# A fused attention and ternary feed-forward kernel on one core: the last group's first MLP placed inside the sixth group's third stage, the f1 bias products in two parts, the last norm's variance in one-input passes, and a new order of all engines

## The reference

```python
x = x + attn(layernorm(x))
x = x + ffn(layernorm(x))

def attn(x):                                   # 256 features, 64 for Q and K
    n = layer_norm(x) * ln1_w + ln1_b
    Q, K = elu(n @ q_w.T + q_b) + 1, elu(n @ k_w.T + k_b) + 1
    V = n @ v_w.T + v_b
    a = causal_linear_attention(Q, K, V)       # sum over earlier tokens, divided by sum(q * k)
    x = x + a @ o_w.T + o_b
    h = gelu((layer_norm(x) * ln2_w + ln2_b) @ f1_w.T + f1_b)   # exact gelu
    return x + h @ f2_w.T + f2_b               # f1: 256 -> 1024, f2: 1024 -> 256

def ffn(x):
    h = gelu(x @ absmean(W_fc).T)              # absmean: weights of -1, 0 and 1
    h = layernorm(h) * ln_w + ln_b             # over 1024 features
    return h @ absmean(W_proj).T
```

## Time and profile before

| | us |
|---|---|
| median of 3 runs | 448.62 (448.35 to 449.17) |
| profiled execution, its own time | 450.32 |
| span of the profiled execution | 448.5 |
| PE busy in the span | 425.4 |
| before the first matmul | 6.42 |
| from the last matmul's end to the end of the span | 7.8 |

### The profile page before, as it was taken

The page is one execution under the profiler, slowest core; times in us unless marked ns, Lnnn a source line. Parts: engine busy times, 40 slices in busy tenths (PEclk is TensorE's granted clock), DMA queues, the critical chain, the costliest instruction groups (busy, mean ns, idle before and its releaser), DMA issues. The chain is left out here.

```text
span 448.5 us, 9187 instructions
## 1 busy us (share of the span) xinstructions
PE 425.4 (95%) x2910; PEld 388.0 (87%) x2910; DVE 361.1 (81%) x1156; ACT 324.6 (72%) x578; POOL 300.5 (67%) x268
## 2 busy tenths in 40 slices
PE   4999999999999999999999999999999999999892
PEld 3888888988989898988999899898989998989782
DVE  6797996886897888968897889978797858946686
ACT  4889558987498758986588847988388857963490
POOL 3684068596778559876689946895878521677384
PEclk9999998999999999999999999999999999999897
DMA  7324030100410021020301120120300000010011
GB/s 241 124 95 142 0 96 1 31 20 0 142 47 3 1 94 50 0 96 11 87 0 48 50 71 2 41 79 1 95 1 2 1 1 0 1 48 3 1 47 50
DMA packets 13521, 20.44 MB, mean 46 GB/s; under 512 B 2720, under 2 KB 11040, under 8 KB 12960
## 3 DMA queue, kind: packets, MB, share of 16 engines
q1 hardware_dynamic: 13472, 19.84, 13.7%
HBM read 15.62 MB, written 4.22 MB: 44 GB/s over the span
## 5 line engine op out<-in xcount | busy, mean ns | idle before, releaser
L1475 POOL TENSOR_TENSOR h<-h 128x512 f32<-128x512 f32 x56 | 72.5, 1295 | 8.8 <-ACT h L851 4.2
L292 PE MATMUL bank_y<-wf_hi,h_hi 128*128 128x256 f32 x224 | 63.4, 283 | 0.8 <-DVE h_lo L1091 0.6
L551 PE MATMUL bank_y<-wpj_t,g_hi 128*128 128x256 f32 x256 | 63.3, 284 | 0.1
L294 PE MATMUL bank_y<-wf_hi,h_lo 128*128 128x256 f32 x224 | 62.6, 279 | 0.0
L293 PE MATMUL bank_y<-wf_lo,h_hi 128*128 128x256 f32 x224 | 62.6, 279 | 0.0
L551 PE MATMUL bank_y<-wpj_t,g_lo 128*128 128x256 f32 x256 | 62.2, 280 | 0.0
L1453 POOL TENSOR_TENSOR rs<-ve,neg_half 128x2 f32<-128x2 f32 x32 | 22.5, 703 | 49.7 <-DVE ve L1028 45.8
L1091 DVE TENSOR_TENSOR h_lo<-bank_f,h_hi 128x512 fp32r<-128x512 f32 x45 | 30.5, 686 | 26.1 <-ACT h_hi L806 25.9
L551 PEld LDWEIGHTS bank_y<-wpj_t,g_hi 128*128 128x128 f32 x256 | 48.1, 188 | 2.2 <-issue 0.5
L551 PEld LDWEIGHTS bank_y<-wpj_t,g_lo 128*128 128x128 f32 x256 | 48.2, 188 | 1.2
L797 ACT ACTIVATE bank_f<-bank_f,f_bias 128x512 f32<-128x512 f32 x48 | 31.6, 662 | 20.0 <-PE bank_f L294 19.6
(11 more groups left out here) (330 smaller groups left out, 1471.3 us busy)
## 6 DMA issues: line engine op xcount, KB each, us to landing
out<-y_yc SPq DMA_DIRECT2D x15, 256.0 KB, 2.3
lines_b<-lines SPq DMA_DIRECT2D x6, 512.0 KB, 3.9
u<-in_xt SPq DMA_DIRECT2D x6, 512.0 KB, 3.6
x_even<-in_x SPq DMA_DIRECT2D x8, 256.0 KB, 2.9
x_odd<-in_x SPq DMA_DIRECT2D x8, 256.0 KB, 3.0
h<-in_f SPq DMA_DIRECT2D x1, 1024.0 KB, 7.7
y_yc<-in_f SPq DMA_DIRECT2D x1, 1024.0 KB, 10.0
h<-in_fc SPq DMA_DIRECT2D x1, 1024.0 KB, 6.1
```

Of the source, the lines that this page charges most:

```text
L292: pe.matmul(ps, w[0], r[0], start=start, stop=False, skip_group_check=skip)
L294: return pe.matmul(ps, w[1], r[0], start=False, stop=stop, skip_group_check=skip)
L551: mm = pe.matmul(out_half(t), gr[part][:, (8 * g + m) % RG, t * P:(t + 1) * P], wpj[:, m, :], start=(m == 0 and part == 0 and t % 2 == 0), ...
L1475: pool.tensor_tensor(squares[:, 0, :], squares[:, 0, :], square_tile(m), ALU.add).then_inc(s["squares_sum"], 1)
```

## The change

Five things are changed.

1. `fill` is gone. `f1b` has two parts: part 0 (m = 0 to 4, ten matmuls) stands where `fill` stood, part 1 (m = 5 to 7, six matmuls) behind `scores(0)`. `f1_bias_add` has two parts as well. `v_mm(0, 0)` now waits for the first of them, and the load of W_proj waits for part 1, which ends earlier than `f1b` did.
2. At ACT's start the gelu table is touched once and the order is another: a further table load (exp) stands ahead of `qk_exp(0)`, and all four `abs_part` stand ahead of the second `z2_norm` of group 0. The `gelu_table` call of group 6 is gone.
3. The ring goes by slot numbers. For groups 0 to 5 they are the same. Group 7's eight f1 tiles now stand between fc tiles 3 and 4 of group 6; fc tiles 4 and 5 follow in the middle of f2(7), tile 6 behind its first half, tile 7 behind its second. `tsq(6)` writes another bank.
4. The last norm: `square` scales by 1/32, so that the sum of the 1024 squares is their mean. A new `ln4_mean` (four operations for the mean and four for its square less eps) stands right behind `h_sum`, and `ln4_var` has four operations in place of twelve; the four of the mean in `centre(g, 0)` are gone.
5. All five lists are written in another order. In groups 1 to 7 the attention tiles and `tz3` of the group before now alternate: `attend(g, 0)`, `tz3(g-1, 0)`, `attend(g, 1)`, `tz3(g-1, 1)`, `attend(g, 2)` (in group 1 `tz3(0, 0)` and `tz3(0, 1)` lie round `attend(1, 3)`).

The diff, cut to its core:

```diff
+        def f1_slot(g, m):
+
+            return 18 * g + m - (0 if g < G - 1 else KH - EARLY)
+
+        def z3_slot(g, h):
+
+            return 18 * g + 8 + h
+
+        def fc_slot(g, m):
+
+            return 18 * g + 10 + m + (KH if g == G - 2 and m >= EARLY else 0)
...
+        def square_bank(g):
+
+            return bank_a[0] if g == G - 2 else bank_a[1]
...
-            def f1b():
-                pe.wait_ge(s["f1_loaded"], 16)
-                pe.wait_ge(s["vec_loaded"], 16)
-                pe.wait_ge(s["v_lo"], 1)
-                for m in range(KH):
+            def f1b(part):
+                if part == 0:
+                    pe.wait_ge(s["f1_loaded"], 16)
+                    pe.wait_ge(s["vec_loaded"], 16)
+                else:
+                    pe.wait_ge(s["v_lo"], 1)
+                for m in (range(FIRST), range(FIRST, KH))[part]:
                     for k in range(KD):
                         mm = pe.matmul(bank_y[0][:, m * BW:(m + 2) * BW], f1_raw[:, k, m * P:(m + 1) * P],
                                        ln2b_c[:, k:k + 1].to_broadcast([P, 2 * BW]),
@@ -390,13 +411,6 @@
                                 k == 0, k == KD - 1)
                 mm.then_inc(s["qk_done"], 1)
 
-            def fill():
-
-                pe.wait_ge(s["wqk_hi"], KD)
-                pe.wait_ge(s["wf1_hi"], 1)
-                for _ in range(10):
-                    pe.matmul(bank_y[1][:], wqk[0][:, 0, :], wf1[0][:, 0, 0:512], start=True, stop=True)
-
...
+                    if h == 0:
+                        pe.wait_ge(s["f1_bias_ready"], 1)
...
+            def slot_free(n):
+
+                for g in range(G):
+                    for m in range(KH):
+                        if f1_slot(g, m) == n - 3:
+                            pe.wait_ge(s["h_lo"], 8 * g + m + 1)
+                        if fc_slot(g, m) == n - 3:
+                            pe.wait_ge(s["g_lo"], 8 * g + m + 1)
+                            pe.wait_ge(s["h_added"], 8 * g + m + 1)
...
-                        pe.wait_ge(s["f1_bias_ready"], 1)
+                        pe.wait_ge(s["f1_bias_ready"], 2)
...
             def tsq(g):
 
                 pe.wait_ge(s["squares_sum"], 7 * g + 7)
-                pe.wait_ge(s["z2_lo"], 2 * min(g + 1, G - 1) + 1)
+                if g != G - 2:
+                    pe.wait_ge(s["z2_lo"], 2 * min(g + 1, G - 1) + 1)
+                else:
+                    pe.wait_ge(s["h_total"], g + 1)
                 for t in range(T):
-                    mm = pe.transpose(bank_a[1][:, t * P:(t + 1) * P], squares[:, 0, t * P:(t + 1) * P], ident[:])
+                    mm = pe.transpose(square_bank(g)[:, t * P:(t + 1) * P], squares[:, 0, t * P:(t + 1) * P], ident[:])
                 mm.then_inc(s["sq_done"], 1)
 
             def ths(g):
 
                 pe.wait_ge(s["h_added"], 8 * g + 8)
-                pe.wait_ge(s["xa_ready"], 4 * min(g + 1, G - 1) + 2)
+                pe.wait_ge(*((s["xa_ready"], 4 * g + 6) if g < G - 1 else (s["h2_total"], G - 1)))
...
-                qkb(); tu(0, 0); tu(0, 1); wvo_mm(); qk_mm(0); bvo(); fill(); tu(1, 0); v_mm(0, 0); v_mm(0, 1)
-                tu(1, 1); scores(0); qk_mm(1); attend(0, 0); attend(0, 1); attend(0, 2); attend(0, 3); f1b()
...
+                qkb(); tu(0, 0); tu(0, 1); wvo_mm(); qk_mm(0); bvo(); f1b(0); v_mm(0, 0); tu(1, 0); v_mm(0, 1)
+                tu(1, 1); scores(0); f1b(1); qk_mm(1); attend(0, 0); attend(0, 1); attend(0, 2); attend(0, 3)
...
+                fch(6, 1, 1); fch(6, 1, 0); fc(6, 2); attend(7, 3); fc(6, 3); proj(6, 0); proj(6, 1); tz2(7, 0)
+                proj(6, 2); tz2(7, 1); proj(6, 3); f1h(7, 0, 0); f1h(7, 0, 1); f1h(7, 1, 1); f1h(7, 1, 0); f1(7, 2)
+                f1(7, 3); f1(7, 4); f1(7, 5); f2(7, 0, 1); f2(7, 1, 1); f1(7, 6); f1(7, 7); f2(7, 0, 0); f2(7, 1, 0)
+                fc(6, 4); fc(6, 5); f2(7, 2, 0); f2(7, 3, 0); f2(7, 4, 0); f2(7, 5, 0); f2(7, 6, 0); f2(7, 7, 0)
+                fc(6, 6); f2(7, 2, 1); f2(7, 3, 1); f2(7, 4, 1); f2(7, 5, 1); f2(7, 6, 1); f2(7, 7, 1); fc(6, 7)
+                proj(6, 4); proj(6, 5); tz3(7, 0); ths(6); tz3(7, 1); proj(6, 6); tsq(6); fch(7, 0, 0); fch(7, 0, 1)
+                proj(6, 7); fch(7, 1, 0); fch(7, 1, 1); fc(7, 2); fc(7, 3); proj(7, 0); fc(7, 4); proj(7, 1); fc(7, 5)
+                proj(7, 2); fc(7, 6); proj(7, 3); fc(7, 7); proj(7, 4); proj(7, 5); proj(7, 6); ths(7); tsq(7)
+                proj(7, 7)
...
-                if g == 0 and m == 0:
-                    act.wait_ge(s["f1_bias_ready"], 1)
-                act.activation(f1_bank(m)[:], f1_bank(m)[:], ACT.Gelu, bias=f1_bias[:, m:m + 1]).then_inc(s["h_gelu"], 1)
+                if g == 0 and m in (0, FIRST):
+                    act.wait_ge(s["f1_bias_ready"], 1 if m == 0 else 2)
...
-                act.activation(square_tile(m), fc_bank(m)[:], ACT.Square).then_inc(s["squared"], 1)
+                act.activation(square_tile(m), fc_bank(g, m)[:], ACT.Square, scale=1.0 / 32).then_inc(s["squared"], 1)
...
+                tables(); gelu_table(); ln3_hi(); wqk_hi(); u_norm(0, 0); u_norm(0, 1); u_hi(0, 0); u_hi(0, 1)
+                wvo_copy(); wf1_hi(0); wf1_hi(1); wf1_hi(2); qk_exp(0); wvo_hi(); u_norm(1, 0); u_norm(1, 1); qk_hi(0)
...
-            def f1_bias_add():
-                dve.wait_ge(s["f1b_done"], 1)
-                dve.tensor_tensor(f1_bias[:], bank_y[0][:, 0:KH * BW:BW], f1b_c, ALU.add).then_inc(s["f1_bias_ready"], 1)
+            def f1_bias_add(part):
+                ms = (slice(0, FIRST), slice(FIRST, KH))[part]
+                dve.wait_ge(s["f1b_done"], part + 1)
+                dve.tensor_tensor(f1_bias[:, ms], bank_y[0][:, ms.start * BW:ms.stop * BW:BW], f1b_c[:, ms],
+                                  ALU.add).then_inc(s["f1_bias_ready"], 1)
...
                 dve.wait_ge(s["sq_done"], g + 1)
                 if g:
                     dve.wait_ge(s["ln4_ve"], 4 * g)
-                dve.tensor_reduce(h2_total[:], bank_a[1][:].rearrange("p (t f) -> p t f", t=T),
+                dve.tensor_reduce(h2_total[:], square_bank(g)[:].rearrange("p (t f) -> p t f", t=T),
                                   AXX, ALU.add).then_inc(s["h2_total"], 1)
 
             def h_sum(g):
 
+                dve.wait_ge(s["hs_done"], g + 1)
                 if g:
                     dve.wait_ge(s["h_mean"], 4 * g)
-                    dve.wait_ge(s["h_mean2"], 4 * g)
-                dve.wait_ge(s["hs_done"], g + 1)
                 dve.tensor_reduce(h_total[:], bank_a[0][:].rearrange("p (t f) -> p t f", t=T),
                                   AXX, ALU.add).then_inc(s["h_total"], 1)
 
+            def ln4_mean(g):
+
+                dve.wait_ge(s["h_total"], g + 1)
+                if g:
+                    dve.wait_ge(s["centred"], 4 * g)
+                    dve.wait_ge(s["ln4_ve"], 4 * g)
+                for t in range(T):
+                    dve.tensor_scalar(h_mean[:, t:t + 1], h_total[:, t:t + 1], -1.0 / H, None, ALU.mult).then_inc(s["h_mean"], 1)
+                dve.wait_ge(s["h_mean"], 4 * g + 4)
+                for t in range(T):
+                    dve.tensor_scalar(h_less[:, t:t + 1], h_mean[:, t:t + 1], h_mean[:, t:t + 1], LN_EPS,
+                                      ALU.mult, ALU.subtract).then_inc(s["h_less"], 1)
+
             def ln4_var(g):
 
-                dve.wait_ge(s["h_total"], g + 1)
-                for t in range(T):
-                    dve.tensor_scalar(h_mean2[:, t:t + 1], h_total[:, t:t + 1], h_total[:, t:t + 1], -1.0 / (H * H),
-                                      ALU.mult, ALU.mult).then_inc(s["h_mean2"], 1)
                 dve.wait_ge(s["h2_total"], g + 1)
-                dve.wait_ge(s["h_mean2"], 4 * g + 4)
+                dve.wait_ge(s["h_less"], 4 * g + 4)
                 if g:
                     dve.wait_ge(s["ln4_rs"], g)
                 for t in range(T):
-                    dve.tensor_scalar(ve[3][:, t:t + 1], h2_total[:, t:t + 1], 1.0 / H, h_mean2[:, t:t + 1],
-                                      ALU.mult, ALU.add).then_inc(s["h_var"], 1)
-                dve.wait_ge(s["h_var"], 4 * g + 4)
-                for t in range(T):
-                    dve.tensor_scalar(ve[3][:, t:t + 1], ve[3][:, t:t + 1], 0.0, LN_EPS, ALU.max, ALU.add).then_inc(s["ln4_ve"], 1)
+                    dve.tensor_scalar(ve[3][:, t:t + 1], h2_total[:, t:t + 1], h_less[:, t:t + 1], LN_EPS,
+                                      ALU.subtract, ALU.max).then_inc(s["ln4_ve"], 1)
 
             def centre(g, t):
...
 
-                if t == 0:
-                    dve.wait_ge(s["h_total"], g + 1)
-                    if g:
-                        dve.wait_ge(s["centred"], 4 * g)
-                    for n in range(T):
-                        dve.tensor_scalar(h_mean[:, n:n + 1], h_total[:, n:n + 1], -1.0 / H, None, ALU.mult).then_inc(s["h_mean"], 1)
...
+                h_add(7, 7); g_lo(7, 7); h_sum(7); ln4_mean(7); h2_sum(7); centre(7, 0); ln4_var(7); centre(7, 1)
```

(1 more changed line is left out.)

557 lines of the change are left out of this document (270 added, 287 removed).

## The result

The changed kernel takes 451.65 us (median of 4 runs, 450.81 to 451.99), the kernel before beside it 448.80 (448.35 to 449.17). The ratio is 1.0059, with a 95% interval of 1.0042 to 1.0075: it is slower by 0.6%, where 445.5 and so faster was forecast; it lies above the whole stated range, which ended at 450.5. The profiled execution took 451.74 us with a span of 449.9; of before it was 450.32 and 448.5.

What follows compares the result with a forecast made beforehand. PE was taken as the bound, busy 425.4 of 448.5 us. Terms -0.3 - 1.2 - 1.6 + 1.1 - 1.1 = -3.1 took the median 448.62 to 445.5 (own range 443.3 to 447.6; whole range 441.5 to 450.5).

Steps and rivals of the forecast that it cites:

- The first term: Start of the kernel: PE idle time added, partly given back later; sum -0.3 us, between -2.5 and +4.
- The hole: Start, group 0: PE idle from about 30.6 to 34.9 us waiting for ACT's z2, then some 1.5 more; +2.7 us.
- the half clock at 66 to 74 us: Slow matmuls behind a 1.1 us wait for z3, expected to go as attend(1, 3) fills the wait; 1.7 us.
- the third term: Last two groups up to gelu3(7, 0): interleaved work covers waits and slow clock, new waits open; -1.6 us, bounds -4 to +1.
- The second term: Middle groups: alternating attention and tz3 covers waits at 170.12 and 374.52; -1.2 us, between -2.7 and +0.3.
- The fourth: Last stage: POOL is the bound, with ln4_rstd(6), two outputs and seven sq_add in its chain; +1.1 us, 0 to +3.
- The fifth: Tail from tsq(7) to the last output: fewer small operations ahead of the power; -1.1 us, between -1.5 and -0.4.
- the slow one: Start: PE leaves the idle time at 30.6 to 34.9 at half clock; start +4, total 449.8 us; chance 0.17.
- The table rival: Start: ACT stands as long again behind the new load ahead of qk_exp(0), about 1.3 later; 446.8 us; chance 0.05.

## Why the prediction was wrong

**The first term, the start: -0.3 forecast, +4.0 in the traces.** Its first half held. The hole was forecast at 30.6 to 34.9 and came at about 30.8 to 35.0 in two waits; the first f1h was forecast at 40.8 and came at 41.08. Part 0 of f1b hid in the wait for wvo_lo, and `v_mm(0, 0)` came 0.40 later, for 0.15 to 0.25. What failed is the sentence on what is given back: "one new wait for `h_lo` of 0.45 remains: -1.1". By `f1(0, 7)` 1.2 of the 3.0 were indeed given back; then 4.2 were lost up to `f2(0, 7, 1)`. The run with ternary(3) moved has the same PE order, no wait and no fall of the clock, and takes 7.0 us there; the changed kernel takes 11.3. Of these 4.3, 2.65 are the wait of 2.50 with its restart and 1.66 the half clock behind it. The walk, that is the new lists gone through call by call with the durations of before, had priced the ternary calls by the time they took before, 2.05 each, where nothing ran on POOL; in the changed kernel they take 2.97, 2.97 and 2.91. The trace of before had no row of this operation beside a large POOL operation, and the step named no queue behind the three calls on DVE. The runs bear this out: ternary(3) moved gives 3.3 us, POOL's xs(0) moved gives 2.1. Both the longer calls and their place in the queue are needed for the wait: one call moved out of the queue ended it though the others stayed slow (2.20 for a select), and as the three are 2.7 us longer in all, the wait of 2.50 would be near nothing with the old durations too, by my estimate from these rows. Moving abs_part, the other suspect, made it slower.

**In the same term, the half clock at 66 to 74 us: -1.7 forecast as given back.** It cannot be counted against the median. The profiled execution of before had it and took 450.32; more than half of the executions of that program took some 1.5 us less, and the median of those shown was 1.7 lower. I had taken the difference between traces as one that carries over to the medians. The same holds for the 1.4 of slow clock in the third term. With the two at nothing the prediction's own sum is 0.0, and 448.6 for the median. The two events are the likeliest reason why the traces differ by 1.4 and the medians by 2.85; a profile shows one execution, and a clock event in it has to be seen in a second before it stands in a sum. It also cuts the other way: against the run with the start of before, whose clock stayed up, the changed start is 4.8 late at `v_mm(2, 0)`, not 4.0. And the four executions of before beside the changed kernel, 448.80, were all of the faster kind; over the 69 of later the median is 449.38, which makes the loss 2.3 us.

**The second term, the middle: -1.2 forecast, -0.3 in the traces**, and +0.1 by the two kernels that differ in it alone. The -0.3 hold the new variance too, which alone gives about 1.0 in this stretch (252.8 for 253.9); so the new order by itself cost 0.7 to 0.9 there. The wait of 0.76 at 170.12 went and one of 0.39 for v_lo came in its place, in front of the same attend. With the old variance the middle is slower by up to 4.7; the forecast had no such dependence.

**The third term, the last groups up to gelu3(7, 0): -1.6 forecast, -2.0 measured.** The two waits at tz3(7, ...) came at 0.48 and 0.46 for 0.7 and 0.55, that at fc(6, 3) at 0.24 for 0.75, that at proj(6, 1) at 0.35 for 0.27, and those at tz2(7, 1) and z3_lo did not show: 1.5 in all for 3.05. That the sum comes so near is luck: it counts 1.4 of slow clock as given back, but before, the clock fell only from `fch(7, 0, 0)` on, behind the stretch that the -2.0 measure, and the 1.5 of waits that did not come stand in for it.

**The fourth, the last stage: +1.1 forecast, +0.5 measured**, and POOL is its bound, with `tsq(7)` released by POOL. The 0.5 are against a stage of before with half clock in it; against the two runs whose clock stayed up it is +1.0 (17.8 for 16.8). From ln4_rstd(6) to the last sum of squares POOL took 15.7 for a forecast of 15.8. fc(7, 3) waited 0.78 for a forecast of 1.3. (The working has a slip: 424.6 + 15.8 is 440.4, not 440.1.)

**The fifth, the tail: -1.1 forecast, -0.8 measured.** y_cpj ended at 443.63 and the variance at 443.84, so that it was just in time, where 0.1 to 0.2 late was forecast.

Of the rivals, the slow one named the right part of the kernel and nearly the right price (+4 for the start, though its terms add up to 3.7), but another mechanism, and that its price is near is luck: it had half clock after the hole. The clock did fall there (0.66 over 30 to 40), but it cost little, about 0.55 us (2.45 from `tz2(0, 1)` to the first f1h for 1.90 before), for up to there ACT set the time and not PE; the forecast had put it at 0.4. The table rival is out: the load ahead of `qk_exp(0)` ran from 15.37, and the activation started at 16.66, 1.29 later, with nothing in between. The Trainium skill's 1283 ns for a load ("ScalarE: Activation LUTs", "What ACT_TABLE_LOAD costs") agrees with the 1.28 here; of the drain of about 1380 ns that it adds, nothing is seen on either side of this load, as ACT's work before it ended at 15.35.

What stays open: what the hole costs by itself, which no run removed; which waits make the rest of the 4.7 us of the run with only the middle; and what decides, at one and the same wait of 1.05 at 70.25, whether an execution falls to half clock.

## What to carry to other kernels

When a change moves long operations of one engine together, price them by what runs beside them on the other engines in the new order and by who starts first, and look who is queued behind them; a walk with the old durations finds the waits that were there, not those that the move makes. Changes that are useless or harmful alone (here an interleaving at +0.8 and a shorter chain of small operations at -0.8) can be worth 2.4 us together, so test them in pairs before one is dropped. And where a profile shows a clock event, look whether other executions have it before its cost is put in the sum.

## What the hardware showed that was not expected

- DVE's compare and select operations on 128 x 1024 tiles in fp32 and POOL's adds on 128 x 512 tiles slow each other: 0.74 to 1.59 or 1.72 and 1.28 to 2.19 on DVE, 2.5 to 3.0, 3.1 and 4.1 for two operations on POOL. The one that starts first kept its time in the pairs read here (compare 0.74 with the add at 1.85; add 1.29 with the compare at 1.72). DVE's h_lo, with one input in PSUM, kept 1.28 for two beside the same adds, and ACT's activations in the same stretch kept their durations.
- The clock fell to half behind a wait of 2.50 us (0.55 from 63.3 to 67.0) and of 1.93 us (0.65 from 424.7 to 429.0), and did not behind one of 1.72 us; behind one of 1.05 us it fell in two profiled executions of the same start and did not in five, and behind 1.05 and 0.64 at the same end it fell in two (0.58 and 0.71 over 3 us) and did not in two.
